# A Mamba-style scan and a quantised matmul on one core: C products in tiles of 64 rows, three more states by B diagonals, and small work moved between engines

## The reference

```python
x = x + s6(layernorm(x))                       # selective scan, 16 states per channel
x = x + quantized_matmul(layernorm(x)) + bias  # int8 rows, int8 weights, 512 to 512

def s6(x):
    xp = x @ x_proj_w.T                        # 64 ranks, then B (16), then C (16)
    delta = softplus(xp[..., :64] @ dt_proj_w.T + dt_proj_b)
    # for each channel d and state n, along the 2048 steps:
    #   h = exp(delta * A[d, n]) * h + delta * B[n] * x[d];   y[d] += C[n] * h
    return y + x * D
```

## Time and profile before

| | busy, us | share | instructions |
|---|---|---|---|
| PE | 2736.5 | 99% | 22612 |
| PE weight loads | 2519.7 | 91% | 22612 |
| DVE | 2705.4 | 98% | 2801 |
| ACT | 2690.0 | 97% | 4927 |
| POOL | 2691.9 | 98% | 981 |

### The profile page before, as it was taken

One profiled execution on the slowest core, in us unless ns is written; L12 is line 12 of the kernel. 1 busy time (PEld: TensorE's weight loads), 2 busy tenths in 40 slices (PEclk: granted clock), 3 DMA queues, 4 the chain that ended last, 5 costly groups with the idle time before them and its releaser, 6 DMA issues.

```text
span 2760.5 us, 59331 instructions
## 1 busy us (share of the span) xinstructions
PE 2736.5 (99%) x22612; PEld 2519.7 (91%) x22612; DVE 2705.4 (98%) x2801; ACT 2690.0 (97%) x4927; POOL 2691.9 (98%) x981
## 2 busy tenths in 40 slices
PE   8999999999999999999999999999999999999998
PEld 7999999999999999999999999999999999999987
DVE  7999999999999999999999999999999999999987
ACT  8999999999999999999999999999999999999995
POOL 5899999999999999999999999999999999999998
PEclk9999999999999999999999999999999999999999
DMA  6345446355454454464554544544545535445452
GB/s 198 100 101 139 123 116 148 107 124 133 118 142 117 120 142 123 116 143 112 124 131 116 145 112 117 149 112 127 137 118 124 127 117 149 111 113 154 99 133 54
DMA packets 271654, 344.35 MB, mean 125 GB/s; under 512 B 174917, under 2 KB 174917, under 8 KB 251018
## 3 DMA queue, kind: packets, MB, share of 16 engines
q1 hardware_dynamic: 250538, 275.54, 34.0%
q0 software_dynamic: 20832, 65.02, 13.8%
HBM read 253.60 MB, written 103.16 MB: 129 GB/s over the span
## 4 chain that ended last, share of the span: by engine, by line
PE 97%; DVE 1%; ACT 1%; issue 0%; DMA 0%; SPq 0%; DVEq 0%; POOL 0%; ACTq 0%
PE Y L855 32%; PE PB L830 23%; PE PB L833 21%; PE Y L851 4%; PE PM L962 4%; PE PM L921 4%; PE PM L902 4%; PE PM L892 2%; PE PM L930 2%; DVE A L994 1%; PE PM L909 0%; ACT A L669 0%; ACT DB L688 0%; PE PM L872 0%; PE PM L879 0%
## 5 line engine op out<-in xcount | busy, mean ns | idle before, releaser
L604 POOL TENSOR_TENSOR A<-A,CB 128x2048 f32<-128x2048 f32 x511 | 2342.0, 4747 | 42.4 <-ACT CAR L676 40.9
L994 DVE TENSOR_TENSOR_SCAN A<-A,CAR,PB 128x512 f32<-128x512 f32 x1536 | 1828.9, 1260 | 9.9 <-ACT A L669 4.6
L669 ACT ACTIVATE A<-DEL,an 128x512 f32<-128x512 f32 x2048 | 1332.5, 713 | 6.3 <-PE Y L855 5.8
L855 PE MATMUL Y<-idf,A 128*128 128x128 f32 x8192 | 1085.1, 273 | 0.0
L855 PEld LDWEIGHTS Y<-idf,A 128*128 128x128 f32 x8192 | 932.7, 141 | 6.5 <-issue 0.5
L688 ACT ACTIVATE DB<-XN,BC 128x512 f32<-128x512 f32 x1344 | 891.7, 711 | 3.6 <-DVE XN L1024 3.6
L833 PE MATMUL PB<-idf,DB 128*128 128x128 f32 x5376 | 764.1, 273 | 8.4 <-DVE A L994 7.0
L830 PEld LDWEIGHTS PB<-DG,XN 128*128 128x128 f32 x5632 | 685.9, 192 | 70.8 <-issue 48.3
L830 PE MATMUL PB<-DG,XN 128*128 128x128 f32 x5632 | 726.7, 276 | 2.5 <-DVE A L994 2.4
L833 PEld LDWEIGHTS PB<-idf,DB 128*128 128x128 f32 x5376 | 621.7, 141 | 66.3 <-issue 39.5
L994 DVE TENSOR_TENSOR_SCAN A<-A,PB 128x512 f32<-128x512 f32 x512 | 584.8, 1201 | 12.5 <-PE PB L833 7.4
(11 more groups left out here) (94 smaller groups left out, 1407.0 us busy)
## 6 DMA issues: line engine op xcount, KB each, us to landing
CB<-c_rows SPq DMA_DIRECT2D x128, 1024.0 KB, 4.8
DG<-b_diag SPq DMA_DIRECT2D x192, 256.0 KB, 5.0
X<-in_x SPq DMA_DIRECT2D x31, 1024.0 KB, 7.3
out<-X SPq DMA_DIRECT2D x31, 1024.0 KB, 5.2
out<-bias_rows POOLq DMA_DIRECT2D x31, 1024.0 KB, 8.8
out<-C POOLq DMA_DIRECT2D x31, 1024.0 KB, 12.7
b_diag<-DG SPq DMA_DIRECT2D x2, 1536.0 KB, 10.7
b_diag<-BC SPq DMA_DIRECT2D x192, 2.0 KB, 5.4
```

Of the source, the lines that this page charges most:

```text
L604: gp.tensor_tensor(A[s % NA][:, :, :], A[s % NA][:, :, :], CB[:, s % (4 * NG), :].unsqueeze(1).broadcast_to([128, KB, L]), ALU.mult).then_ ...
L669: act.activation(A[s % NA][:, g, :], DEL[k % 2][:, g, :], ACT.Exp, scale=an[:, g, n:n + 1])\
L855: i = pe.matmul(Y[j][:, g * 128:(g + 1) * 128], A[s % NA][:, g, j * 128:(j + 1) * 128], idf[:, :], is_transpose=True, start=False, stop=(n ...
L994: dve.tensor_tensor_scan(A[s % NA][:, g, :], A[s % NA][:, g, :], PB[(4 * s + g) % NPB][:, :], init, ALU.mult, ALU.add).then_inc(s_scan, 1)
```

## The change

The C products are taken in halves: 64 channels (array rows) and 64 output columns each, the two halves of a channel group into two different accumulator banks, so the four banks Y become one array YR of two tile pairs by two halves. The gather on DVE then reads eight pieces of 256 columns, and a small addition joins the two row sums. Twelve more blocks go by diagonals: 34 instead of 22, nine states instead of six. The first norm's statistics become a sum and a sum of squares about the mean on ACT, in place of `bn_stats` and `bn_aggr`; its rows are all made on POOL. The centring of the second norm moves from POOL to ACT, with its shift made beforehand (`step2`). The small operations of the scales (`ascale`, `step`) and the shift of the first norm move from POOL to DVE. All places are new.

```diff
-PERIOD = 1000
+PERIOD = 10000
 PLACES = {
...
-        "add_b": (1370,),
+        "add_b": (13072,),
...
-        "carry": (32, 51, 110, 154, 208, 294, 329, 354, 528, 560, 594, 645, 663, 754, 829, 932),
-        "centre": (1370, 1370, 1371, 1380),
+        "carry": (1220, 1667, 2525, 3374, 3831, 4015, 4733, 5403, 6679, 6926, 7437, 7825, 8433, 8844, 9646,
+        10271),
+        "centre": (16889, 17290, 17372, 17544),
...
-        "delta": (-462, -443, -424, -401),
+        "delta": (-3141, -2825, -2638, -2495),
...
-        "load_g": (35, 113, 310, 426, 1034, 1035),
+        "load_g": (-1347, -759, -60, 168, 631, 640, 659, 1751, 5865),
...
-        "put_x": (1260,),
+        "put_x": (15423,),
...
-        "store_c": (79,),
-        "store_g": (33,),
+        "store_c": (-7224,),
+        "store_g": (-5187,),
...
-        "times_c": (97, 119, 170, 204, 212, 222, 259, 290, 576, 582, 661, 679, 682, 731, 867, 933),
-        "turn": (1884,),
+        "times_c": (-4528, -3748, -925, 335, 1714, 1947, 2142, 2333, 2337, 2681, 2832, 2923, 3726, 3836, 3978,
+        4274),
+        "turn": (12139,),
...
-    ROWS = {2: 4, 5: 4, 8: 4, 11: 4, 14: 4, 15: 2}
+    ROWS = {1: 4, 3: 4, 5: 4, 7: 4, 8: 2, 9: 4, 11: 4, 13: 4, 15: 4}
...
-        Y = [ps(f"Y{i}", [128, D]) for i in range(T)]
+        YR = ps("YR", [128, T // 2, 2, D])
+        Y = [YR[:, i // 2, i % 2, :] for i in range(T)]
...
             def th(k, i):
                 n, j = divmod(i, T)
                 s = NS * k + n
+                at = [[YR[:, j // 2, r, 256 * (j % 2) + 64 * g:256 * (j % 2) + 64 * g + 64] for r in range(2)] for g in range(KB)]
+                half = [slice(64 * r, 64 * r + 64) for r in range(2)]
...
                     for g in range(KB):
-                        i = pe.matmul(Y[j][:, g * 128:(g + 1) * 128], XT[:, g, j * 128:(j + 1) * 128], dd[:, g, :],
-                                      start=(g == 0), stop=False, skip_group_check=True)
+                        for r in range(2):
+                            i = pe.matmul(at[g][r], XT[half[r], g, j * 128:(j + 1) * 128], dd[half[r], g, half[r]],
+                                          start=(g == 0 and j % 2 == 0), stop=False, skip_group_check=True)
                     i.then_inc(s_dy, 1)
                 for g in range(KB):
-                    i = pe.matmul(Y[j][:, g * 128:(g + 1) * 128], A[s % NA][:, g, j * 128:(j + 1) * 128], idf[:, :],
-                                  is_transpose=True, start=False, stop=(n == NS - 1), skip_group_check=True)
+                    for r in range(2):
+                        i = pe.matmul(at[g][r], A[s % NA][half[r], g, j * 128:(j + 1) * 128], idf[half[r], half[r]],
+                                      is_transpose=True, start=False, stop=(n == NS - 1), skip_group_check=True)
                 i.then_inc(s_th, 1)
...
-            def gather(p, j):
-                dve.wait_ge(s_th, 4 * NS * (p + 1) - 3 + j)
-                if j == 0 and p >= 1:
+            def gather(p, i):
+                j, r = divmod(i, 2)
+                if r == 0:
+                    dve.wait_ge(s_th, 4 * NS * (p + 1) - 3 + (j | 1))
+                    if j == 0 and p >= 1:
+                        dve.wait_ge(s_sum, p)
+                channels = X[p % NX][:, j, :].rearrange("p (g r c) -> p r g c", g=KB, r=2)[:, r, :, :]
+                dve.scalar_tensor_tensor(channels, YR[:, j // 2, r, 256 * (j % 2):256 * (j % 2) + 256]
+                                         .rearrange("p (g c) -> p g c", g=KB), 1.0, channels, ALU.mult, ALU.add,
+                                         accum_out=SY[:, r, j:j + 1]).then_inc(s_y, 1)
...
+            def sum1(p, j):
...
+                act.activation(XN[p % 2][:, j, :], X[p % NX][:, j, :], ACT.Copy, accum_out=L1[:, 0, j:j + 1]).then_inc(s_s1, 1)
+
+            def sq1(p, j):
+                act.wait_ge(s_s1, T * p + j + 1)
+                act.activation(XN[p % 2][:, j, :], X[p % NX][:, j, :], ACT.Square, bias=L1[:, 0, j:j + 1], scale=-float(D),
+                               accum_out=L1[:, 1, j:j + 1]).then_inc(s_s2, 1)
...
+            def centre(p, j):
...
+                    act.wait_ge(s_st, p + 1)
+                act.activation(CQ[:, j * D:(j + 1) * D], X[p % NX][:, j, :], ACT.Identity, bias=AM[:, 0, j:j + 1],
+                               scale=AM[:, 3, j:j + 1]).then_inc(s_c, 1)
...
+            def step2(p):
+                dve.wait_ge(s_s3, p + 1)
+                dve.wait_ge(s_nm, p + 1)
+                dve.tensor_tensor(AM[:, 0, :], AM[:, 3, :], SX[:, 1, :], ALU.mult).then_inc(s_st, 1)
```

More of the change, by code:

```diff
@@ new lines @@
+        "idle": (200000, 200001, 200002, 200003),
+        "inv": (15111,),
+        "last_p": (200000, 200001),
+        "last_q": (200000, 200001, 200002, 200003),
+        "last_v": (200000, 200001),
+        "late": (200000, 200001, 200002, 200003),
+        "load": (-19854,),
+        "load_c": (-1688, -87, 890, 2040),
+        "load_g": (-1347, -759, -60, 168, 631, 640, 659, 1751, 5865),
+        "log0": (-7188,),
+        "put_last": (200000, 200001, 200002, 200003),
+        "put_x": (15423,),
@@ new lines @@
+        "q_mm": (19486, 20353, 20865, 21130),
+        "q_t": (200000, 200001, 200002, 200003),
+        "qt_out": (18702, 19803, 21184, 22161),
+        "root": (15587,),
+        "rstd0": (-6802,),
+        "scale_a": (20123, 21177, 21615, 22140),
+        "scale_out": (200000, 200001, 200002, 200003),
+        "scale_p": (16399,),
+        "scales": (16900,),
+        "scan": (893, 899, 946, 1038, 1057, 1089, 1197, 1197, 1197, 1197, 1365, 1579, 1579, 1938, 2378, 2794,
[5 rows of a table added]
+        "square": (14083, 14242, 14705, 14775),
@@ L104 @@
-        "delta": (-74157, -60979, -54203, -54032),
-        "dl_t": (-24857, -24740, -24740, -24089),
-        "du": (-1253, -1155, -842, -842),
-        "gather": (1098, 1111, 1111, 1119),
-        "inv": (1208,),
-        "late": (-12995, -12985, 100, 200),
-        "load": (16363,),
-        "load_c": (-27496, -8988, -6862, 534),
-        "load_g": (-26047, -9268, -8644, -7488, -7488, -7486),
-        "log0": (-125282,),
-        "put_x": (1491,),
-        "q_mm": (1852, 1858, 1871, 1900),
-        "qt_out": (1693, 1755, 1788, 1796),
@@ new lines @@
+        "delta": (-51446, -51129, -47664, -44284),
+        "dl_t": (-53833, -48092, -46188, -46131),
+        "du": (-46034, -46033, -44734, -36293),
+        "gather": (11817, 11876, 11969, 11996, 12054, 12054, 12083, 12111),
+        "inv": (15306,),
+        "late": (-56200, -56100, 1000, 2000),
+        "load_c": (-56600, -87, 890, 2040),
+        "load_g": (-56500, -56400, -56300, -56000, 631, 640, 659, 1751, 5865),
+        "log0": (-63754,),
+        "put_x": (14136,),
+        "q_mm": (19402, 20268, 20604, 20912),
@@ new lines @@
+        "q_mm": (19377, 19995, 20164, 20642),
+        "q_t": (13366, 16749, 18943, 19647),
+        "qt_out": (24130, 24245, 25861, 30679),
+        "root": (20340,),
+        "rstd0": (-6854,),
+        "scale_out": (20817, 21232, 23842, 23909),
+        "scales": (16342,),
+        "scan": (854, 907, 907, 907, 919, 925, 949, 980, 993, 993, 1154, 1501, 1583, 1921, 2005, 2295, 2324,
[5 rows of a table added]
+        "square": (14083, 16427, 16506, 17346),
+        "step": (16887,),
+        "step2": (16968,),
+        "store_c": (-3690,),
```

392 lines of the change are left out of this document (169 added, 223 removed), and 86 rows, old and new, of tables (FIRST, LAST, PLACES).

## The result

The changed kernel takes **3226.2 us** (median of four runs, 3221.8 to 3229.8) where the kernel before takes 2763.5: a ratio of 1.1675, 95% interval [1.1658, 1.1691]. I had forecast 2742 with a range up to 2796. It is 463 us slower, some 15 us a chunk.

The account below looks back on a forecast made before the run. All four engines were taken as full, PE bounding at 84.43 us a chunk; PE falling to 83.75 gave -22.3 us over 31 chunks, start and end +0.5, so 2742 us from a median of 2764.1; range 2716 to 2796.

Parts of the forecast that it names:

- the one on DVE: Eight small operations moved to DVE add 0.6 us a chunk, within a DVE sum of -2.0.
- The second rival: SP's queue: put_x behind turn and nine stores delays POOL, a round of 82.2 to 85.4 us; up to 2794; chance 0.20.
- the loads: SP's queue: three more diagonal stores and 256 KB loads a chunk, about 3x(0.5+0.4) us, costed at nothing outside one rival.
- The steps on PE: PE a chunk: diagonals +5.5, C products -13.1, turns +6.9, sum -0.7 us, to 83.75.
- A pair: PE's C products: two half passes load and stream together in 0.058 us, saving 13.1 us a chunk.
- The turns: PE's changes of array shape around 22 runs of C products a chunk: +6.9 us, lower bound 0.
- The first rival: PE's turns cost little, PE falls to 77 us and ACT bounds: 2735 down to 2722; chance 0.16.
- the third: PE's half loads queue, 0.116 us a pair, +14.8+3.5 us a chunk: 3310; chance 0.10.
- start and end: Start: ACT +1.0 and norms on POOL +0.8; end: halved C products -1.3; together +0.5 us.
- Gathers: DVE: eight gathers of 0.33 us in place of four of 0.6, +0.2 us a chunk.
- The fourth rival: All engines: the new order's stalls eat the gain, 0.7 us more a chunk, 2758 to 2769; chance 0.10.
- The forecast's own sign of failure: Mechanism is wrong if PE idles, or POOL waits for put_x, by over 2 us a chunk.

Follow-up runs that it names:

- d_one: Changed kernel with its small VectorE operations as runs of 128x1 operations, the sum of the halves' moments as a tensor_reduce: 2969.8 us (1.075).
- e_load_only: d_one with the last diagonal's load issued on SP ahead of the turn and stores, put_x left in place: 2970.0 us (1.075).
- f_reduce: d_one with put_x and the last diagonal's load ahead of the turn, and 20 of 24 width-1 operations a chunk as six tensor_reduces: 2756.1 us (0.9976).
- h_half: Kernel before with C and skip products in half tiles, eight gathers, and one tensor_reduce for the halves' moments: 2790.5 us (1.010).
- b_wide: Kernel before with two idle one-source tensor_scalars a chunk on VectorE, the first 128x4, the second 128x1: 3041.4 us (1.101).
- b_probe: Kernel before with two idle 128x4 operations a chunk on VectorE, a two-source tensor_tensor and a one-source tensor_scalar: 3070.6 us (1.112).
- b_single: Kernel before with an idle 128x4 reciprocal and a 128x1 multiplication by per-partition scalars a chunk on VectorE: 2769.5 us (1.002).

## Why the prediction was wrong, step by step

**The step that failed** is the one on DVE: "Eight small operations at an aggregate's 0.08: +0.6", with "each wait would cost about as much as an operation again" as the only bound. Three of the eight took 6.3, 4.5 and 2.4 us on average, 13 us a chunk in place of 0.6 for all. I priced them by their shape, from an operation with one source, and never asked what they read and who reads beside them. The upper bound was missing: where the trace has no row for such an operation on such an engine, it lies with the longest thing that it could wait for, POOL's 4.55 us, or two of them; the probes stood for up to 9.6. This step cost 256 us by d_one; the operations' own share and the clock's were not parted.

**The second rival had the right queue and the wrong round.** put_x behind nine stores holds POOL up, 261.3/31 = 8.4 us a chunk. The record had 0.95 us a chunk at the top end (its price halfway, 2775, should by its own terms be 2768). The runs show (2970.0-2815.7)/31 = 5.0, once the load beside it is moved. The rival's own condition, over 6.5 us for nine stores, is not met: they took 4.8 to 6.2 us, the turn's issue some 1.9 and not 4.4; put_x landed 6.1 us after its issue, not 5.2. By the record's sum such a round takes some 81 us and costs nothing. The round that closes is another one. In e_load_only:

```profile
1566.17 0.90 POOL L623 DMA_DIRECT2D out<-bias_rows  x1 [8.30 <-DMA out<-X]
...
1608.83 3.49 POOL L579 TENSOR_SCALAR XN<-X,SM 128x512 f32<-128x512 f32 x4
...
1612.37 0.66 PE L901 MATMUL PM<-idf,XN 128*128 128x128 f32 x4 [1.14 <-POOL XN L579]
...
1641.32 0.81 ACT L792 ACTIVATE C<-X,AM 128x512 int16<-128x512 f32 x1
...
1642.16 1.79 SPq L511 DMA_TRANSPOSE C<-C  x1
...
1651.32 0.50 SPq L504 DMA_DIRECT2D out<-X  x1
...
1657.47 0.90 POOL L623 DMA_DIRECT2D out<-bias_rows  x1 [8.76 <-DMA out<-X]
```

Behind the bias addition POOL works for 46.2 us, not 18.9, to the end of the next first norm's rows (eight C multiplications, the column scaling, four norms). PE has stood for these rows; its projection, the B products behind it, the scan before state 10's carry, and on ACT that carry, two scalings, a delta and a table load come ahead of the last centring, which ends 29.8 us later. Then 9.2 us to put_x's issue and 6.2 to the next bias addition: 91.3 us, the chunk of this kernel. The record closed the round through 33 scans and counted the delta's work, not what the delta and the carry wait for.

**What I costed at nothing** was the loads: "if that cover goes, PE's diagonal of state 15 is late". It went, for a reason that the profile of before gives: there six stores alone take 5.45 us of SP's queue, and the ninth load stands behind all nine. The consequence was named, the condition not worked out. It decides together with put_x.

**The steps on PE held, but for 0.7 us.** A pair costs 0.0625 us, where I took 0.058 between 0.058 and 0.116. It shows in the weight loads of the changed kernel:

```profile
1484.82 1.07 PEld L865 LDWEIGHTS YR<-idf,A 64*128 64x128 f32 x32 [0.17 <-issue]
1485.96 0.42 PEld L839 LDWEIGHTS PB<-idf,DB 128*128 128x128 f32 x4
1486.55 0.57 PEld L865 LDWEIGHTS YR<-idf,A 64*128 64x128 f32 x16 [0.17 <-issue]
1487.19 0.42 PEld L839 LDWEIGHTS PB<-idf,DB 128*128 128x128 f32 x4
```

From its first load to the next work, a run of 32 half passes takes 1485.96-1484.82 = 1.14 us, one of 16 1487.19-1486.55 = 0.64: 0.50 for eight pairs. The turns come out of the same rows. Out: 0.64-8x0.0625 = 0.14. In: from 1485.96 to 1486.55, 0.59 for four passes that take 0.44, 0.15. The record had 0.153 and 0.149, from one product of 1 row. The first rival (turns cost little) and the third (the loads queue) are thereby out. The instructions of PE came to 33242 for some 33400.

With the pairs at 0.0625 PE has 1.15 us a chunk more than forecast, 84.9. f_reduce's turns start at 434.66 and, 24 chunks later, at 2454.42, so a chunk takes 84.16, 0.7 less, which I can't place. It is 0.31 us a chunk under the kernel before, not 0.72: some 10 us in all, of which start and end, forecast at +0.5, take 3.5 back. Its 2756.1 is 14 us over my 2742: with the waits gone PE bounds, as forecast, and the gain is 7 us, not 22. The terms of PE's sum that offset each other were not tested one by one.

**Gathers** were mis-sized too: 8x0.344-4x0.61 = +0.31 us a chunk by their starts, not +0.2, and VectorE had the least to spare in h_half.

**The fourth rival** (the new order's stalls eat the gain) was the right kind of thought, at 0.7 us a chunk for 15. The forecast's own sign of failure, POOL waiting for put_x by over 2 us a chunk and PE idling by over 2, is what the profile showed first.

## What to carry to other kernels

Before an operation moves to VectorE, ask whether it reads two SBUF tensors, or is a tensor_scalar on more than a column (128x4 here), and what GpSimd runs meanwhile; a tiny one then costs up to two of GpSimd's instructions, 9.6 us here. A reduce over interleaved rows or single columns did the same work here without standing. And when several things are late at the same point, moving one shows nothing: 12 and 0 us alone were 154 together, so test pairs before calling a cause harmless.

## What the runs showed of the hardware that I had not expected

- A 128x4 fp32 tensor_scalar with one source stands behind GpSimd as a two-tensor sum does: 7405 and 7402 ns on average in the same place. 128x1 took 154, a reciprocal 161, a tensor_reduce of 128x8 136.
- The standing outlasts the instruction that runs: it passed from one multiplication to the next, up to 9.6 us in b_wide, and ended within 0.03 us of the end of a POOL instruction in all 94 cases of the changed kernel.
- With VectorE standing for 7 us a chunk TensorE's clock is 0.953 on average (b_probe, where TensorE idles for 178 of the stage's 2027 us); with the reciprocal in the same place it is 1.000 (b_single, 4 us).
- Two 64-row halves load and stream at once: 0.0625 us a pair, 0.109 for the full pass; changing to them and back costs 0.15 and 0.14 us.
